# A graph layer with a GRU and a gated feed-forward: tiles of 128 rows in place of 125

## The reference

```python
h = ln(x)
m = relu(concat([h[src], edge_attr]) @ W1.T + b1) @ W2.T + b2   # 2500 x 512
agg = segment_sum(m, dst, 10000)
gi, gh = agg @ W_ih.T + b_ih, h @ W_hh.T + b_hh                 # 10000 x 1536
r, z = sigmoid(i_r + h_r), sigmoid(i_z + h_z)
n = tanh(i_n + r * h_n)
h_new = (1 - z) * n + z * h
x = x + h + gamma * (h_new - run_mean) * rsqrt(run_var + eps) + beta
g = ln(x)
# 8 small experts of width 32, the two best of each row, and a shared one of width 32
x = x + sum_e comb[:, e] * (relu(g @ eW1[e] + eb1[e]) @ eW2[e] + eb2[e]) + 0.5 * shared(g)
```

## Time and profile before

| what | value |
|---|---|
| median of 3 runs | 1486.32 us (1485.1 to 1486.37) |
| profiled execution, its time | 1488.01 us |
| profiled execution, its span | 1486.2 us |
| TensorE busy | 1400.7 us, 94% |
| VectorE, GpSimd, ScalarE busy | 1109.3, 926.5 and 609.7 us |
| DMA queue of SP | 32048 packets, 73.48 MB |
| DMA queue of POOL | 45056 packets, 79.02 MB |
| granted clock of TensorE, mean | 0.98 |

### The profile page before, as it was taken

The page is one execution under the profiler, slowest core; times in us unless marked ns, Lnnn a source line. Parts: engine busy times, 40 slices in busy tenths (PEclk is TensorE's granted clock), DMA queues, the critical chain, the costliest instruction groups (busy, mean ns, idle before and its releaser), DMA issues. The chain is left out here.

```text
span 1486.2 us, 23121 instructions
## 1 busy us (share of the span) xinstructions
PE 1400.7 (94%) x6780; PEld 1138.9 (77%) x6780; DVE 1109.3 (75%) x2777; ACT 609.7 (41%) x1100; POOL 926.5 (62%) x1049
## 2 busy tenths in 40 slices
PE   4699999999679999999999999999999999999995
PEld 3578888877457888888888888888888888888884
DVE  3475444234278888888888888888888888888885
ACT  3341212201244445444445444454444454444441
POOL 3210250302178787878787877878788878787771
PEclk9899999999889999999999999999999999999997
DMA  8312333345522223332223222233322223322220
GB/s 215 124 52 91 113 116 123 104 123 149 176 92 98 88 93 103 100 103 93 90 97 102 99 96 91 96 101 103 103 93 90 94 102 100 103 92 91 96 91 28
DMA packets 77137, 152.92 MB, mean 103 GB/s; under 512 B 34842, under 2 KB 36744, under 8 KB 76979
## 3 DMA queue, kind: packets, MB, share of 16 engines
q0 software_dynamic: 45056, 79.02, 16.7%
q1 hardware_dynamic: 32048, 73.48, 15.2%
HBM read 115.67 MB, written 36.66 MB: 103 GB/s over the span
## 5 line engine op out<-in xcount | busy, mean ns | idle before, releaser
L1453 PE MATMUL bank<-whh_hi,h_hi 128*125 128x512 f32 x960 | 391.7, 408 | 22.2 <-DVE h_lo L486 22.2
L1453 PE MATMUL bank<-whh_hi,h_lo 128*125 128x512 f32 x960 | 379.5, 395 | 0.0
L1453 PE MATMUL bank<-whh_lo,h_hi 128*125 128x512 f32 x960 | 378.2, 394 | 0.0
L1453 PEld LDWEIGHTS bank<-whh_hi,h_hi 128*125 128x125 f32 x960 | 178.8, 186 | 60.1 <-DVE h_lo L486 22.6
L1453 PEld LDWEIGHTS bank<-whh_hi,h_lo 128*125 128x125 f32 x960 | 178.3, 186 | 44.6
L1453 PEld LDWEIGHTS bank<-whh_lo,h_hi 128*125 128x125 f32 x960 | 178.8, 186 | 37.9
L1210 POOL DMA_INDIRECT gates<-gates_in,slot_at x80 | 129.7, 1622 | 78.3 <-POOL slot_at L1208 65.4
L1291 ACT ACTIVATE hn_raw<-bank 125x512 f32<-125x512 f32 x80 | 47.8, 598 | 270.6 <-PE bank L1453 270.6
L1249 POOL TENSOR_TENSOR h_n<-h,n_gate 125x512 f32<-125x512 f32 x80 | 103.8, 1297 | 59.5 <-ACT n_gate L1319 59.5
L1235 POOL TENSOR_TENSOR hn<-hn_raw,hn_bias 125x512 f32<-125x512 f32 x80 | 104.1, 1301 | 31.0 <-ACT hn_raw L1291 30.9
L1262 POOL TENSOR_TENSOR x_h_b<-x_h,bn_shift 125x512 f32<-125x512 f32 x80 | 104.2, 1303 | 20.8 <-ACT x_h L479 18.0
(11 more groups left out here) (176 smaller groups left out, 3290.0 us busy)
## 6 DMA issues: line engine op xcount, KB each, us to landing
xt<-in_x SPq DMA_DIRECT2D x80, 250.0 KB
out<-y SPq DMA_DIRECT2D x80, 250.0 KB
gates_in<-g_out SPq DMA_DIRECT2D x16, 750.0 KB
wih_lo_raw<-in_wih_t SPq DMA_DIRECT2D x4, 768.0 KB, 24.9
whh_lo_raw<-in_whh_t SPq DMA_DIRECT2D x4, 768.0 KB, 11.8
gates_in<-late_out SPq DMA_DIRECT2D x6, 250.0 KB
gates_in<-g_out SPq DMA_DIRECT2D x6, 250.0 KB
gates<-gates_in,slot_at POOLq DMA_INDIRECT x80, 10.8
```

Of the source, the lines that this page charges most:

```text
L1453: last = pe.matmul(to[0:R, :], a[:, s, k * R:(k + 1) * R], w[:, k, q * D:(q + 1) * D], start=n == 0, stop=n == 3 * DK - 1)
```

## The change

The host's part pads: x gets rows of zeros up to 10112 = 128 x 79, and the edges get 60 more (source 0, attributes 0, and as destination row 10112, which no node has) up to 2560 = 128 x 20. `R` is 128 everywhere, `SW` is 512, the node stage has 79 tiles, and the output's first 10000 rows are returned. Since the wider tiles take more of the on-chip memory, `paired` and two pieces of the feed-forward weights (`f2_last`, `f2_last_hi`) are put where buffers lie that are no longer used. The last wait takes an odd number of tiles into account. Everything else, the order of the instructions on each engine included, is the same; the loop has 18 turns as before, and five periods stand behind it.

```diff
-    assert N == R * NT and EC == SUP * NSUP and HE == (KF - 1) * P and 3 * V <= P and NT % 2 == 0
+    assert N == R * NT and EC == SUP * NSUP and HE == (KF - 1) * P and 3 * V <= P
...
-    paired = place("paired", [R, GE, 8, 8])
+    paired = nc.alloc_sbuf_tensor_at("paired", [R, GE, 8, 8], F32, offset=at_all)
+    assert at_all + 4 * GE * 64 <= region_rows
...
-    f2_last = place("f2_last", [P, D])
-    f2_last_hi = place("f2_last_hi", [P, D], F32R)
+
+    f2_last = nc.alloc_sbuf_tensor_at("f2_last", [P, D], F32, offset=region_bias)
+    f2_last_hi = nc.alloc_sbuf_tensor_at("f2_last_hi", [P, D], F32R, offset=region_bias + 4 * D)
...
-                sp.wait_ge(y_stored[s], 16 * (NT // 2))
+                sp.wait_ge(y_stored[s], 16 * ((NT + 1 - s) // 2))
...
-    rows, edge_tiles, sup = 125, 20, 4
+
+    rows, sup = 128, 4
+    x = np.asarray(x)
+    nodes = x.shape[0]
+    x = np.concatenate([x, np.zeros((-nodes % rows, x.shape[1]), x.dtype)])
     src, dst, attr = np.asarray(src), np.asarray(dst), np.asarray(edge_attr_128)
+    more = -src.shape[0] % (rows * sup)
+    edge_tiles = (src.shape[0] + more) // rows
+    src = np.concatenate([src, np.zeros(more, src.dtype)])
+    dst = np.concatenate([dst, np.full(more, x.shape[0], dst.dtype)])
+    attr = np.concatenate([attr, np.zeros((more, attr.shape[1]), attr.dtype)])
...
-    return result.results[0]["out"]
+    return result.results[0]["out"][:nodes]
```

## The result

The kernel with 128 rows takes 1439.97 us (median of 4 runs, 1438.56 to 1442.45) against 1485.84 us before (4 runs), a ratio of 0.9694 with an interval of [0.9682, 0.9707]: faster by 45.9 us. The profiled execution took 1442.45 us with a span of 1440.6, 45.6 less than the span before.

What follows compares the result with a forecast made beforehand. It took TensorE to bound the node stage, and the edge stage except for stalls behind slow 125-row DMA. Terms -13.2 + 2.8 + 1.3 - 8.3 - 3.5 - 13.2 - 1.2 = -35.3 us gave a 1451.0 us median, range 1442 to 1465.

Steps and rivals of the forecast that it cites:

- One tile fewer: Node stage: one node tile less saves one period of 13.16 us, taken from the periods behind the loop; -13.2 us.
- Wider operands on TensorE: Edge-stage matmuls go from 500 to 512 columns, +2.8 us (bounds +2.5, +3.7); three more rows cost nothing readable.
- The rival of the weight loads on the path: Three more columns per weight load, paid at node-tile and some edge matmuls: +13.3 us, 1464.3 us in all; chance 0.07.
- DVE and ACT, and the pace of a tile: Operation L1369, awaited by the expert layer, takes 16 ns more at 512 columns, 79 times: +1.3 us; bounds 0 and +3.2.
- DMA, the first 65 us: Edge-stage start: broadcasts on 16 engines bring x rows and group 1 attributes earlier, ending two stalls; -8.3 us, bounds -5, -10.
- The last group: Edge stage's last group: stores finish earlier, so POOL's gathers start 6.4 us sooner; -3.5 us, bounds -1.9 and -3.9.
- The passage: Between edge and node stages: stores land about T0 + 3 (T0: DVE's last addition ends), TensorE resumes T0 + 17.1; -13.2 us.
- POOL's start to r_pre 11.5 us: Between the stages: time from POOL's gather start to r_pre, kept at the 11.5 us of the kernel before.
- The end: Kernel's end: SP's 3.7 us wait for the last store shrinks as it drains faster; -1.2 us, bounds 0 and -2.
- a direct transfer of 125 rows runs on five engines: Reading of DMA shares (0.32 for 125-row stores): 125 rows use five engines, 128 rows all 16.
- the same three terms: DMA terms for the first 65 us, the last group and the passage: -8.3, -3.5 and -13.2 us.
- the signs that the forecast named: Profile marks expected after, including passage wait 9 to 11 us, tile 13.15 to 13.19 us, 512-column matmuls at 0.231 us.

## Why the prediction was right in kind and too small

Read term by term from the two profiled executions (forecast, then measured):

- *One tile fewer*: -13.2; 13.2 in the run with 80 tiles. Right.
- *Wider operands on TensorE*: +2.8; from the first to the last matmul of the sums +1.8 (279.3 to 281.1 us). The low bound was 2.5, so a little under it. The rival of the weight loads on the path, 2.5 ns more for each matmul, did not come: the gate matmuls come 2 ns sooner. Since what sets their pace is open, this is no proof that three more rows in the array are free.
- *DVE and ACT, and the pace of a tile*: +1.3; instead the period fell from 13.16 to 13.14 us, and the node stage without its tile, from TensorE's resume to the last h_new, took 2.4 us less. This term has the wrong sign. The wait that it looked at did grow, from 25.7 to 29.0 us. Two things outweighed it that the forecast held fixed. The gate matmuls come every 0.2293 us and no longer every 0.2314, 36 times a tile (0.08 us), though they have three more rows. And the gathers of 128 rows are worth 0.015 us, as the run with gates of 125 rows shows.
- *DMA, the first 65 us*: -8.3, with a bound of -10; the first of the sums starts 10.2 us earlier. Near in size, in part by luck, for the cause is incomplete: in the kernel before, direct transfers spread alone shortened the first stretch by 1.0 us, with DVE waiting 6 us for gathers of 125 rows, and with those split too by 7.9 us. In the changed kernel either of the two at 125 rows costs only about 2 us of this stretch; it is both together that cost 9.
- *The last group*: -3.5, with a bound of -3.9; from the last of the sums to the first node matmul 39.4 us became 35.1, -4.3. The gather waits for the sums, not for stores, as forecast, and at 339.2 us for the forecast 341.
- *The passage*: -13.2; -15.4, inside the bounds of 9 and 16. The stores land at T0 + 2.35 for the forecast 3. The step "POOL's start to r_pre 11.5 us" was kept as before, but it had been set by the gather of 125 rows; it takes 9.9 us now, and DVE's weight chain is what holds it there.
- *The end*: -1.2; the tail behind the last h_new is 1.9 us shorter, and SP's wait 1.6 us for 3.7. The tails of three runs of full tiles differ by 2 us among themselves (23.2, 21.1, 23.5), so no more than its sign can be claimed.

These add up to -45.6 us, the difference of the two spans, where the sum of the forecast was -35.3. Of the 10.3 us between them 3.7 are in the pace of a tile, 2.2 in the passage, 1.9 in the first 65 us, and 2.5 in the other three. Four terms lie past their own low bounds: the wider operands (+1.8 for +2.5), the pace (-2.4 for 0), the first 65 us (-10.2 for -10) and the last group (-4.3 for -3.9). With every term at its low bound the median would have been 1443.7 us, so a time below 1442 is not a matter of a noisy run alone.

Two steps failed.

The first is the term for the pace of a tile. It held TensorE's matmuls at the 0.2309 us of before and let a tile only grow: +1.3 us forecast, -2.4 measured, the largest single error. The matmuls are faster in the changed kernel; why they are is open.

The second is one sentence of the reading, "a direct transfer of 125 rows runs on five engines", taken as if POOL's gathers did not change with it. Every duration that hung on a gather was carried over from before: the landing in the passage, the issue on POOL in each tile, the competition with the loads in the first 35 us. These errors all had the same sign. The run with gathers of 125 rows and direct transfers of 128 is the kernel that the forecast priced. It takes 1447.82 us against 1441.70, within the range; without the 1.4 us of its memset the gathers are worth 4.7 us, nearly half of what was missing. About 1.2 of these (79 x 0.015) are in the pace already. A row that spoke of it was in the forecast's own first group: 301 GB/s at a share of 0.97 is 310 for a full share, where 133 at 0.32 is 416. After the change the same stretch gives 388 / 1.02 = 380, so most of what was missing belonged to the gathers.

The terms were added as if each stood by itself. Had only SP's transfers changed, as the working supposed, 13.5 us would have come from them (the run with all those of the edge stage and the passage split, in which layer 1 also starts 1.0 us later) where -25.0 was forecast for the same three terms.

Of the signs that the forecast named, three failed: the wait in the passage is 7.0 us and not 9 to 11, the tile takes 13.14 us and not 13.15 to 13.19, and the matmuls come every 0.2293 us and not every 0.231.

## What to carry to other kernels

Look at the number of rows of a tile before anything finer: in this kernel 128 and 126 rows run well, 125 badly, and 127 doubles the time, and both the direct transfers and the gathers that have the rows as their outer dimension show it. If a copy must have 125 rows, cut it only where issues are cheap, and look at the gathers beside it: with direct transfers cut alone, DVE's wait for gathered rows grew from 2.0 to 6.0 us here. Before a cause is priced, take it away alone and put it back alone: here the two answers for direct transfers were 13.5 us and 3 to 5 us, because two slow things stood in each other's shadow.

## What was not expected of the hardware

- The pace of one and the same matmul of 512 columns differs between kernels: 0.2293, 0.2314, 0.232 and 0.2338 us from start to start, at full clock and in unbroken rows. Over 36 of them in each of 79 tiles the ends are 13 us apart. A pace read to four digits before a change is no constant of the change.
- A gather of 125 rows of 6 KB: POOL's queue has 36864 packets when 77 of 79 gathers of gates have 125 rows and 15920 when all have 128, that is 272 packets more for each. One tile more of 128 rows adds 144 (16064 - 15920), so 144 stand against 416. Nearly all of the 272 have 4 bytes; a row of 6144 bytes is one packet in both. The landing goes from 5.6 to 10.8 us; with 126 rows it is 6.1.
- With 127 rows the queue has 216320 packets, a gather's issue holds POOL for 2.7 us, and the granted clock averages 0.741; it is 0.50 in the two stretches above, in which TensorE does nothing.
- Executions of one and the same kernel differ by 3 us (1438.56 to 1442.45), and the profiles show where: the granted clock over the span was 0.989 in one and 0.994 in another of the changed kernel. Effects under 2 us can only be read from milestones in the trace.
